# Two-layer graph network: the attention loops written out, gathers that read their row numbers in place, and a small POOL clear after every eight gathers of the second layer

## The chip, the cores and the metric

The kernel runs on one core of one Trainium2 chip. The metric is the device time of one execution in microseconds (us); the number for the kernel before is the median of three runs.

## The reference, cut to what matters

6250 nodes with 64 values each, 200,000 edges (`src`, `dst`, sorted by `dst`), and 64 values per edge. Two layers, each behind a layer norm and a ReLU.

```python
# layer 0: attention over each edge in both directions (400,000 directed edges, 4 heads of 16)
gl, gr = (h @ Wl.T)[src2].reshape(-1, 4, 16), (h @ Wr.T)[dst2].reshape(-1, 4, 16)
score = (att * leaky_relu(gl + gr, 0.2)).sum(-1)
alpha = softmax of score over the edges of one src2 node
out   = segment_sum(gr * alpha[:, :, None], src2)
x = x + gelu(concat(out, h) @ W1.T + b1) @ W2.T + b2
# layer 1: messages
msg = h[src] + edge_attr_64
agg = segment_sum(msg, dst)
x = x + batch_norm(relu(agg @ W1 + b1) @ W2 + b2)
```

Each layer needs one row of 64 values (256 bytes) per edge, picked by a row number that is known only at run time: `gr[dst2]` in layer 0, `h[src]` in layer 1.

## The kernel before, in words

The program is a row of blocks (`prepare`, `sort`, `decode`, `attention`, `attention_nodes`, `messages`, `message_nodes`), written engine by engine with semaphores set by hand. The first three sort the directed edges by node and write the row numbers of all edges into the tile `m.row_of` (128 partitions, one column for each tile of 128 edges), and tables of rows (`gr_table`, `gl_table`) into DRAM. The change touches `attention`, `messages`, and two helpers.

**attention.** 3328 tiles of 128 edges stand in 416 steps of 8 tiles, and the steps in 13 chunks of 32. Step q goes through these hands:

- POOL (line 827) issues 8 indirect DMAs (gathers). Each fetches 128 rows of `gr_table` into `rows[k]`, k = q mod 8 (`U = GATHER_SLOTS = 8` buffers). The row numbers come from `stage[k]`, a small tile of 8 columns.
- SP (lines 837, 842, 843, 851, 858) loads the places of the edges (`place_b`) and the two blocks of left rows (`gl_step`), whose number it reads into a register (L842), reads back the gathered rows of the step 32 earlier (`rows_again`), and, when the 8 gathers of step q have landed, stores them to DRAM (`gr_rows`, L858).
- PE (L882) builds the left rows of each edge with a one-hot matmul, 8 f32 matmuls per step, and for the step 32 earlier sums weighted rows into 8 bf16 matmuls of 204 columns (L889). Its last matmul of step q counts up `s_step`.
- DVE waits for `s_step` and for the gathers, adds left and right rows (L1030, `fore`, counts up `s_z`), weighs the rows of the chunk before (L1035), adds PE's sums into `acc` (L1017), builds one-hots (L1005, L1053), and reduces to scores (L136). Between L1056 and L1062 stands L1009: it copies the 8 row numbers of step q + 7 from `m.row_of` to `stage[(k - 1) % U]` and counts up `s_staged`.
- ACT casts (L967, L969).

Between two chunks DVE, PE and ACT run a scan over the chunk's scores (softmax maxima), lines 1072 to 1135. A step with a score part and a sum part (chunks 1 to 12) is the full one.

POOL may start the gathers of step q when three things have come: the store of step q - 8 has landed (`s_store[k]`), DVE has added the rows of step q - 8 (`s_z` at least q - 7), and DVE has staged the row numbers of step q (`s_staged` at least q + 1):

```python
at_least(pool, s_store[k], j * 16)
at_least(pool, s_z, q - U + 1)
pool.wait_ge(s_staged, q + 1)
```

The steps stand in loops of the hardware: `walk` writes chunks 0 and 1 out and puts chunks 2 to 12 in one loop; `loop` writes the first 8 steps of a chunk out and puts the other 24 in an inner loop of 3 turns. Semaphore values and slices depend on loop registers. POOL has one loop of 51 turns of 8 steps.

**messages.** 1568 tiles of 128 edges stand in 98 groups of 16 tiles, each in two halves of 8 (196 halves). Python loops write all of it out already; only the few groups whose edges reach past one block of nodes run a small loop of the hardware (L1369, L1433). For half h, POOL issues 8 gathers (L1337) from `h2_table` into `rows[h mod 6]` (`U = 6`), with the row numbers in `stage[k]`. It waits for DVE's message of half h - 6 (`s_message` at least h - 5) and for `s_staged` at least h + 1. DVE stages the numbers of half h + 5 (L1386) just ahead of the message of half h (L1421, gathered rows + edge rows), and adds PE's sums into `agg` (L1399, and L1443 in the small loop). PE's matmuls are at L1358, ACT's casts at L1379 and L1381.

## Time and profile before

| | us |
|---|---|
| median of three runs | 9004.02 |
| the three runs | 8930.97, 9004.02, 9032.82 |
| the profiled execution | 9012.64 |
| its span, first to last instruction | 9010.8 |
| first to last gather of attention (L827) | 1127.5 to 6308.1 |
| first to last gather of messages (L1337) | 6676.0 to 8907.0 |
| POOL busy / DVE busy / PE busy | 5385.2 / 5072.6 / 2933.2 |

A time stands for one engine's instruction from start to end. "Idle before" is the time that the engine stood still ahead of it, and what follows `<-` is who ended that. "issue" means that the engine waited for nothing the profile shows, "remote" that the semaphore's sender could not be matched. SPq rows are DMAs issued by SP. The span and the profiled execution differ by 1.84 us, which lie outside the program's own instructions.

### The profile page before, as it was taken

Reading aid. Unit: us, or ns where it says so; the run is one execution under the profiler, and the core shown is the slowest. Engines: PE = TensorE matmul, PEld = TensorE weight load, DVE = VectorE, ACT = ScalarE, POOL = GpSimd, SP = SyncE. Lnnn points to the kernel's source line nnn. Section 1 sums busy time; section 2 is a strip of 40 time slices with the busy share of each in tenths; the row PEclk is TensorE's granted clock in tenths of the full one; section 3 lists DMA queues with packets and bytes.
Section 4 is the critical chain, followed back from the end, with each engine's and each line's share of the span. In section 5 each row is a group of like instructions: output and inputs, shape, how many; then the busy total and the mean of one; then the engine's idle time right before and its main releaser. Section 6 shows DMA issues by size and latency. Waiting matters only on the chain. (4 is left out here: it accounts for less than half of the span.)

```text
span 9010.8 us, 65938 instructions
## 1 busy us (share of the span) xinstructions
PE 2933.2 (33%) x13731; PEld 2480.9 (28%) x13731; DVE 5072.6 (56%) x7913; ACT 1027.4 (11%) x1576; POOL 5385.2 (60%) x4913
## 2 busy tenths in 40 slices
PE   1011122533544333354444334343341112121223
PEld 1011122423434333353333334343220111111112
DVE  9999922745756565575656556564832323333334
ACT  3001100101111111011111101010210101001101
POOL 0000066767777776777777776777036666667774
PEclk9975555555555555555555555555555555555555
DMA  1000022323433333343333333337311111111211
GB/s 30 0 0 0 9 73 65 104 74 85 107 92 93 90 87 85 83 109 91 86 90 88 87 87 91 87 95 71 69 38 44 47 45 48 44 46 46 48 44 31
DMA packets 530967, 588.05 MB, mean 65 GB/s; under 512 B 274126, under 2 KB 277326, under 8 KB 530466
## 3 DMA queue, kind: packets, MB, share of 16 engines
q1 hardware_dynamic: 370066, 421.03, 15.4%
q0 software_dynamic: 156672, 160.75, 11.6%
q10 hardware_dynamic: 3984, 3.89, 0.2%
q14 instruction: 199, 1.63, 0.1%
q8 instruction: 46, 0.75, 0.0%
HBM read 467.65 MB, written 117.55 MB: 65 GB/s over the span
## 5 line engine op out<-in xcount | busy, mean ns | idle before, releaser
L827 POOL DMA_INDIRECT rows<-gr_table,stage x3328 | 3799.1, 1142 | 2345.4 <-DVE stage L1009 1319.7
L882 PE MATMUL bank<-gl_step,hot_t 128*128 128x64 f32 x6720 | 1562.6, 412 | 2205.7 <-issue 1395.0
L882 PEld LDWEIGHTS bank<-gl_step,hot_t 128*128 128x128 f32 x6720 | 1503.1, 327 | 2335.4 <-issue 1660.5
L1337 POOL DMA_INDIRECT message<-h_table,edge_stage x1568 | 1565.3, 998 | 781.8 <-issue 663.3
L1030 DVE TENSOR_TENSOR fore<-bank,rows 128x512 f32<-128x512 f32 x416 | 283.7, 682 | 1472.0 <-remote 803.5
L1358 PE MATMUL bank<-edge_parts,edge_hot 128*128 128x192 bf16 x1568 | 286.4, 363 | 1789.1 <-DVE edge_parts L1428 1201.5
L889 PE MATMUL bank<-parts,hot_sum 128*128 128x204 bf16 x3328 | 681.5, 374 | 484.0 <-issue 403.1
L1358 PEld LDWEIGHTS bank<-edge_parts,edge_hot 128*128 128x128 bf16 x1568 | 202.7, 140 | 1872.7 <-DVE edge_parts L1428 1259.7
L889 PEld LDWEIGHTS bank<-parts,hot_sum 128*128 128x128 bf16 x3328 | 508.3, 159 | 587.1 <-issue 451.0
L967 ACT CAST parts<-terms 128x544 bf16<-128x544 f32 x416 | 268.5, 645 | 2978.7 <-DVE terms L1038 1804.0
L1053 DVE TENSOR_TENSOR hot_sum<-iota_row,place 128x1024 bf16<-128x1024 f32 x416 | 504.5, 1213 | 6.8 <-issue 6.7
L1035 DVE TENSOR_TENSOR terms<-rows_again,weights 128x512 f32<-128x512 f32 x416 | 282.6, 679 | 314.2 <-DMA rows_again<-gr_rows 297.2
L1399 DVE TENSOR_TENSOR agg<-agg,bank 128x192 f32 x98 | 33.8, 345 | 685.0 <-remote 565.9
L1017 DVE TENSOR_TENSOR acc<-acc,bank 128x204 f32 x832 | 297.2, 357 | 175.9 <-issue 93.4
L1443 DVE TENSOR_TENSOR agg<-agg,bank 128x192 f32 x48 | 17.0, 354 | 612.7 <-remote 547.4
L969 ACT CAST parts<-wide 128x544 bf16<-128x544 f32 x416 | 268.4, 645 | 749.0 <-issue 538.6
L607 PE MATMUL bank<-ident,keys 128*128 128x128 f32 x448 | 96.0, 404 | 785.1 <-DVEq L593 697.9
L1379 ACT CAST edge_parts<-bank 128x512 bf16<-128x512 f32 x196 | 114.9, 586 | 1818.9 <-DVE bank L1421 1056.3
L1005 DVE TENSOR_SCALAR hot_t<-place_b,iota_node 128x1024 f32<-128x1024 bf16 x420 | 314.5, 749 | 0.8 <-issue 0.8
L607 PEld LDWEIGHTS bank<-ident,keys 128*128 128x128 f32 x448 | 86.5, 216 | 795.6 <-DVEq L593 703.7
L1050 DVE TENSOR_TENSOR wide<-terms,parts 128x544 f32<-128x544 f32 x416 | 296.9, 714 | 15.2 <-issue 12.2
L1062 DVE TENSOR_TENSOR parts<-wide,parts 128x544 bf16<-128x544 f32 x416 | 296.1, 712 | 0.0
(267 smaller groups left out, 4355.4 us busy)
## 6 DMA issues: line engine op xcount, KB each, us to landing
place_b<-place_rows SPq DMA_DIRECT2D x422, 256.0 KB
gr_rows<-rows SPq DMA_DIRECT2D x416, 256.0 KB
rows_again<-gr_rows SPq DMA_DIRECT2D x416, 256.0 KB
rows<-gr_table,stage POOLq DMA_INDIRECT x3328
edge<-in_edge_attr SPq DMA_DIRECT2D x97, 512.0 KB
gl_step<-gl_table SPq DMA_DIRECT2D x844, 32.0 KB
message<-h_table,edge_stage POOLq DMA_INDIRECT x1568
pen_s<-pen_rows ACTq DMA_DIRECT2D x56, 64.0 KB
```

What stands on the lines that cost most here:

```text
L827: pool.indirect_dma_start(rows[k][:, g, :], None, m.gr_table[:, :], bass.IndirectOffsetOnAxis(stage[k][:, g:g + 1], 0)).then_inc(s_gath[k] ...
L882: last = pe.matmul(bank[slot % LAG][:, g * D:(g + 1) * D], hot_t[slot % LAG][:, g * P:(g + 1) * P], gl_s[slot][:, g // GROUP_TILES, :], st ...
L889: last = pe.matmul(sums_of(slot, g // GROUP_TILES), hot2[slot][:, g, :], parts[slot][:, g, :, :].rearrange("p w f -> p (w f)"), start=g % ...
L1005: dve.tensor_scalar(hot_t[slot][:, :], place_b[place_slot][:, :], m.iota_node[:, 0:1], None, ALU.is_equal).then_inc(s_hot, 1)
L1017: dve.tensor_tensor(sums, sums, sums_of(slot, i), ALU.add).then_inc(s_acc, 1)
L1030: dve.tensor_tensor(z[:, :, :], bank[k % LAG][:, 0:SW].rearrange("p (g f) -> p g f", f=D), rows[k][:, :, :], ALU.add).then_inc(s_z, 1)
L1035: dve.tensor_tensor(terms[:, :, 0:DH], rows2[k % V][:, :, :].rearrange("p g (h f) -> p (g h) f", f=DH), weight.unsqueeze(2).to_broadcast([ ...
L1050: dve.tensor_tensor(rest[:, :, :], terms_by_tile, parts[k % LAG][:, :, 0, :], ALU.subtract).then_inc(s_rest, 1)
L1053: dve.tensor_tensor(hot2[k % LAG][:, :, :], places, at, ALU.is_equal)
L1062: dve.tensor_tensor(parts[k % LAG][:, :, 2, :], rest[:, :, :], parts[k % LAG][:, :, 1, :], ALU.subtract).then_inc(s_parts, 1)
L1337: pool.indirect_dma_start(rows[k][:, e, :], None, m.h2_table[:, :], bass.IndirectOffsetOnAxis(stage[k][:, e:e + 1], 0)).then_inc(s_gath[k] ...
L1358: done = pe.matmul(out[:, 0:3 * D], one_hot[:, e, :], parts[h % 4][:, e, :, :].rearrange("p w f -> p (w f)"), start=first and e == 0, stop ...
```

## The change

1. In `attention` the loops of the hardware are gone: Python loops write out all 416 steps (and the 13 scans) on every engine. Waits compare with constants, slices are fixed. One load of penalties past the last chunk goes too (4 small DMAs of ACT).
2. In both layers the gathers read their row numbers where they lie, one column of `m.row_of` or `m.src`. The `stage` tiles, DVE's copies (L1009, L1386, 423 and 196 of them) and the waits for `s_staged` are gone. The waits for `s_z`, `s_store` and `s_message` stay.
3. In `messages` POOL, after the 8 gathers of each half, clears 256 columns of a spare tile `idle_tile` (128 partitions, f32) that nobody reads: 196 clears. Ahead of each stands a wait on `s_pool`, which POOL itself counts up.

```diff
@@ class Chain
-        self.eng.wait_ge(self.sem, self.turns + self.n)
+        self.eng.wait_ge(self.sem, self.n)
@@ build
+        m.idle = sb("idle_tile", [P, 256], F32)
@@ attention
-    stage = [sb(f"stage{k}", [P, STEP_TILES], I32, ctx) for k in range(U)]
...
-    def loop(eng, part, body):
-
-        body(part, part.c * outer, True)
-        with eng.Fori(part.c * outer + 1, part.c * outer + outer) as j:
-            body(part, j, False)
+    def loop(part, body):
+
+        for i in range(outer):
+            body(part, part.c * outer + i, i == 0)
...
-        for c in range(2):
-            turn(Part(c))
-        with eng.Fori(2, CHUNKS) as c:
-            turn(Part(c))
-        turn(Part(CHUNKS))
+        for c in range(CHUNKS + 1):
+            turn(Part(c))
@@ attention, POOL
-                    pool.wait_ge(s_staged, q + 1)
                     pool.sem_inc(s_pool, 1)
                     for g in range(STEP_TILES):
+                        tile = q * STEP_TILES + g
                         pool.indirect_dma_start(rows[k][:, g, :], None, m.gr_table[:, :],
-                                                bass.IndirectOffsetOnAxis(stage[k][:, g:g + 1], 0)).then_inc(s_gath[k], 16)
-            body(0)
-            with pool.Fori(1, CHUNKS * outer) as j:
+                                                bass.IndirectOffsetOnAxis(m.row_of[:, tile:tile + 1], 0)
+                                                ).then_inc(s_gath[k], 16)
+            for j in range(CHUNKS * outer):
                 body(j)
@@ attention, DVE
-                        at_least(dve, s_gath[(k - 1) % U], (j + (k > 0)) * 16 * STEP_TILES)
-                        stage_of((k - 1) % U, q + U - 1).then_inc(s_staged, 1)
@@ messages, POOL
                 at_least(pool, s_message, h - U + 1)
-                pool.wait_ge(s_staged, h + 1)
                 pool.sem_inc(s_pool, 1)
                 for e in range(HALF):
+                    tile = h * HALF + e
                     pool.indirect_dma_start(rows[k][:, e, :], None, m.h2_table[:, :],
-                                            bass.IndirectOffsetOnAxis(stage[k][:, e:e + 1], 0)).then_inc(s_gath[k], 16)
+                                            bass.IndirectOffsetOnAxis(m.src[:, tile:tile + 1], 0)).then_inc(s_gath[k], 16)
+                pool.wait_ge(s_pool, STEPS + 2 * h + 1)
+                pool.memset(idle[:, 0:256], 0.0).then_inc(s_pool, 1)
@@ messages, DVE
-                    if h + U - 1 < HALVES:
-                        at_least(dve, s_gath[(h - 1) % U], ((h - 1) // U + 1) * 16 * HALF)
-                        stage_of((h - 1) % U, h + U - 1).then_inc(s_staged, 1)
```

DVE, one full step in attention's loop, before:

```order
L1030 TENSOR_TENSOR fore<-bank,rows 128x512
L1035 TENSOR_TENSOR terms<-rows_again,weights 128x32x16
L1038 COPY terms<-weights 128x32
L1005 TENSOR_SCALAR hot_t<-place_b,iota_node 128x1024
L1044 SCALAR_TENSOR_TENSOR fore<-fore 128x512
L1050 TENSOR_TENSOR wide<-terms,parts 128x544
L1053 TENSOR_TENSOR hot_sum<-iota_row,place 128x1024
L1056 TENSOR_TENSOR wide<-fore,att_sb 128x512
L1009 TENSOR_SCALAR stage<-row_of 128x8
L1062 TENSOR_TENSOR parts<-wide,parts 128x8x68
L136 TENSOR_REDUCE scores<-wide 128x32
```

DVE, the same step in the changed kernel (line numbers are its own):

```order
L1016 TENSOR_TENSOR fore<-bank,rows 128x512
L1021 TENSOR_TENSOR terms<-rows_again,weights 128x32x16
L1024 COPY terms<-weights 128x32
L998 TENSOR_SCALAR hot_t<-place_b,iota_node 128x1024
L1030 SCALAR_TENSOR_TENSOR fore<-fore 128x512
L1036 TENSOR_TENSOR wide<-terms,parts 128x544
L1039 TENSOR_TENSOR hot_sum<-iota_row,place 128x1024
L1042 TENSOR_TENSOR wide<-fore,att_sb 128x512
L1045 TENSOR_TENSOR parts<-wide,parts 128x8x68
L136 TENSOR_REDUCE scores<-wide 128x32
```

The staging copy is gone, ninth of the eleven; all else keeps its place.

SP, the first two thirds of one full step in attention's loop, before (ISA rows set registers):

```order
L851 ISA
L851 DMA rows_again<-gr_rows 128x512
L837 ISA
L837 DMA place_b<-place_rows 128x1024
L842 ISA
L842 TENSOR_LOAD blk_i
L842 ISA x2
L843 ISA
L843 DMA gl_step<-gl_table 128x64
L842 ISA
L842 TENSOR_LOAD blk_i
L842 ISA x2
```

SP, the whole of the same step in the changed kernel:

```order
L844 DMA rows_again<-gr_rows 128x512
L830 DMA place_b<-place_rows 128x1024
L835 TENSOR_LOAD blk_i
L835 ISA x2
L836 ISA
L836 DMA gl_step<-gl_table 128x64
L835 TENSOR_LOAD blk_i
L835 ISA x2
L836 ISA
L836 DMA gl_step<-gl_table 128x64
L851 DMA gr_rows<-rows 128x512
```

SP's DMAs keep their order; 18 of its instructions in such a step become 13, since registers no longer count the loop.

POOL, the end of the second layer, before, with what each row waits for:

```order
L1337 DMA message<-h_table,edge_stage 128x64 x7
L1337 DMA message<-h_table,edge_stage 128x64 [waits s_message,s_edge_staged]
L1337 DMA message<-h_table,edge_stage 128x64 x7
L1337 DMA message<-h_table,edge_stage 128x64 [waits s_message,s_edge_staged]
L1337 DMA message<-h_table,edge_stage 128x64 x7
```

POOL, the same place in the changed kernel:

```order
L1313 DMA message<-h_table,src_sb 128x64 x7
L1316 MEMSET idle_tile 128x256 [waits s_pool]
L1313 DMA message<-h_table,src_sb 128x64 [waits s_message]
L1313 DMA message<-h_table,src_sb 128x64 x7
L1316 MEMSET idle_tile 128x256 [waits s_pool]
```

A clear stands between each 8 gathers and the next; the wait for DVE's message of six halves earlier stays at the first gather of each eight.

## Rows read from the trace of the kernel before

**Rows 1.** The page: span, and busy time of each engine.
```profile
span 9010.8 us, 65938 instructions
PE 2933.2 (33%) x13731; PEld 2480.9 (28%) x13731; DVE 5072.6 (56%) x7913; ACT 1027.4 (11%) x1576; POOL 5385.2 (60%) x4913
```

**Rows 2.** Groups of instructions: count | busy us, mean ns | idle before, releasers.
```profile
L827 POOL DMA_INDIRECT rows<-gr_table,stage x3328 | 3799.1, 1142 | 2345.4 <-DVE stage L1009 1319.7 <-issue 1025.1 <-DVE fore L1030 0.3
L1337 POOL DMA_INDIRECT message<-h_table,edge_stage x1568 | 1565.3, 998 | 781.8 <-issue 663.3 <-DVE edge_stage L1386 118.5
...
L1009 DVE TENSOR_SCALAR stage<-row_of 128x8 int32 (+1 forms) x423 | 77.6, 185 | 4.1 <-issue 3.5 <-PEq L646 0.5
```

**Rows 3.** Stretches: length, then each engine's busy time (instructions), clock, DMA share, GB/s.
```profile
1602.00:6308.00 4706.00, 2005.78 (x9312) 1775.86 (x9312) 2817.61 (x5257) 539.54 (x809) 3492.86 (x3016) 0.50 0.37 90
...
6676.00:8907.00 2231.00, 409.36 (x2288) 303.32 (x2288) 761.33 (x1148) 225.08 (x384) 1565.30 (x1568) 0.51 0.19 46
```

**Rows 4.** Waits of POOL: waited for, us in total, times, longest.
```profile
POOL rows L827 <- DVE stage L1009: 1319.7, 25, 963.9
POOL rows L827 <- issue: 1025.1, 3301, 9.5
POOL message L1337 <- issue: 663.3, 1559, 14.9
...
POOL message L1337 <- DVE edge_stage L1386: 118.5, 9, 116.1
```

**Rows 5.** Waits of DVE.
```profile
DVE fore L1030 <- remote: 803.5, 33, 58.2
DVE agg L1399 <- remote: 565.9, 24, 33.8
DVE agg L1443 <- remote: 547.4, 32, 38.0
```

**Rows 6.** Timeline of attention around one stop of POOL: start, length, engine.
```profile
3016.16 0.27 PE L882 MATMUL bank<-gl_step,hot_t 128*128 128x64 f32 x1 [2.53 <-issue]
3016.27 0.95 POOL L827 DMA_INDIRECT rows<-gr_table,stage  x1 [0.31 <-issue]
...
3020.37 0.69 DVE L1030 TENSOR_TENSOR fore<-bank,rows 128x512 f32<-128x512 f32 x1 [42.01 <-remote]
...
3025.86 0.16 DVE L1009 TENSOR_SCALAR stage<-row_of 128x8 int32 x1
...
3026.20 0.35 SPq L858 DMA_DIRECT2D gr_rows<-rows  x1
...
3026.80 0.95 POOL L827 DMA_INDIRECT rows<-gr_table,stage  x1 [9.58 <-DVE stage L1009]
```

**Rows 7.** Timeline of attention where DVE is busy, gathers of POOL.
```profile
3040.13 2.35 POOL L827 DMA_INDIRECT rows<-gr_table,stage  x1 [0.30 <-issue]
3042.79 0.95 POOL L827 DMA_INDIRECT rows<-gr_table,stage  x1 [0.30 <-issue]
```

**Rows 8.** Timeline of messages around one stop of POOL.
```profile
7486.88 2.74 PE L1358 MATMUL bank<-edge_parts,edge_hot_more 128*128 128x192 bf16 x16 [1.70 <-issue]
...
7517.96 0.95 POOL L1337 DMA_INDIRECT message<-h_table,edge_stage  x1 [0.30 <-issue]
7524.54 0.35 DVE L1443 TENSOR_TENSOR agg<-agg,bank 128x192 f32 x1 [37.71 <-remote]
...
7524.89 0.69 DVE L1421 TENSOR_TENSOR bank<-message,edge 128x512 f32<-128x512 f32 x1
...
7525.75 0.95 POOL L1337 DMA_INDIRECT message<-h_table,edge_stage  x1 [6.84 <-issue]
```

**Rows 9.** POOL's clears and the row behind, start to end of the program.
```profile
0.72 0.20 POOL L334 MEMSET ident<- 128x128 f32 x1 [0.29 <-POOLq L1594]
...
6547.80 7.93 POOL L1192 MEMSET agg<- 128x9408 f32 x1
6555.69 4.21 POOL L1193 CAST dst_f<-dst_sb 128x1568 f32<-128x1568 int32 x1
```

**Rows 10.** DVE at the turn of a chunk loop.
```profile
3171.36 1.01 DVE L1133 COPY weights<-bank 128x512 f32<-128x512 f32 x1 [1.89 <-issue]
3175.47 0.69 DVE L1030 TENSOR_TENSOR fore<-bank,rows 128x512 f32<-128x512 f32 x1 [3.11 <-issue]
```

More of the change, by code:

```diff
@@ L102, in __init__ @@
     def __init__(self, eng, sem):
-        self.eng, self.sem, self.n, self.turns = eng, sem, 0, 0
+        self.eng, self.sem, self.n = eng, sem, 0
     def link(self, ins):
@@ L865, in turn @@
             def turn(part):
-                loop(sp, part, body)
+                loop(part, body)
                 if part.score:
@@ L870, in turn @@
                     sp.sem_inc(s_sp, 1)
-            walk(sp, turn)
+            walk(turn)
             for q in range(STEPS + LAG + 2 - V, STEPS + LAG + 2):
@@ L940, in turn @@
             def turn(part):
-                loop(pe, part, body)
+                loop(part, body)
                 if part.score:
                     scan(part)
-            walk(pe, turn)
+            walk(turn)
         def half_of_weights(i):
@@ L973, in turn @@
                 if part.sum:
-                    loop(act, part, body)
+                    loop(part, body)
                 if not part.score:
@@ L1006, in hot_of @@
                                   ).then_inc(s_hot, 1)
-            def stage_of(k, q):
-                return dve.tensor_scalar(stage[k][:, :], m.row_of[:, bass.ds(q * STEP_TILES, STEP_TILES)], 0.0, None,
-                                         ALU.add)
             def accumulate(r, slot, i):
@@ L1023, in body @@
                     tile = q * STEP_TILES - part.c * CHUNK_TILES
-                    if not isinstance(tile, int):
-                        tile = nc.s_assert_within(tile, 0, CHUNK_TILES - STEP_TILES, skip_runtime_bounds_check_because=
-                                                  "a chunk's steps are its tiles")
                     dve.wait_ge(s_step, q + 1)
@@ L1135, in scan @@
                 dve.wait_ge(s_weights_act, c + 1)
-            for k in range(U - 1):
-                stage_of(k, k).then_inc(s_staged, 1)
             chain.link(dve.memset(m.acc[:, :, :, :], 0.0))
@@ L1149, in turn @@
                 c = part.c
-                loop(dve, part, body)
+                loop(part, body)
                 if part.sum:
@@ L1157, in turn @@
                 if part.score:
-                    before = chain.n
-                    if not isinstance(c, int):
-                        chain.turns = (c - 2) * SCAN_LINKS
                     scan(part)
-                    if part.sum:
-                        assert chain.n - before == SCAN_LINKS, chain.n - before
-            walk(dve, turn)
+            walk(turn)
 def attention_nodes(m, ctx):
@@ L1305, in messages @@
     edge = [sb(f"edge{k}", [P, 2, HALF, D], F32, ctx) for k in range(V)]
-    stage = [sb(f"edge_stage{k}", [P, HALF], I32, ctx) for k in range(U)]
     hot = [sb(f"edge_hot{k}", [P, HALF, P], BF16, ctx) for k in range(4)]
@@ L1319, in messages @@
     s_rel = sem("s_dst_rel")
+    idle = m.idle[:, :]
     def steps_before(eng, g):
@@ L1384, in _ @@
         def _(dve):
-            def stage_of(k, h):
-                return dve.tensor_scalar(stage[k][:, :], m.src[:, h * HALF:(h + 1) * HALF], 0.0, None, ALU.add)
             def hot_of(out, numbers, to, n):
@@ L1399, in add_first @@
                 dve.tensor_tensor(sums, sums, bank[g % 2][:, 0:3 * D], ALU.add).then_inc(s_agg, 1)
-            for k in range(U - 1):
-                stage_of(k, k).then_inc(s_staged, 1)
             dve.tensor_copy(bank[3][:, 0:P], m.iota_row[:, :]).then_inc(s_rel, 1)
```

17 lines of the change are left out of this document (7 added, 10 removed).

## Prediction

> **What bounds the kernel now.** I read the page first [rows 1]: POOL and DVE are busy for 5385 and 5073 of 9011 us, neither all through. The stretches [rows 3] say where: from 1602 to 6308 POOL is busy for 3493 of 4706 us and DVE for 2818, in messages POOL for 1565 of 2231 and DVE for 761. So POOL's 4896 gathers lead both layers, and the groups [rows 2] give their price: 1142 ns each in attention, 998 in messages, with 0.30 us ahead of nearly each. Undisturbed, a gather takes 0.95 us and the next starts 0.30 later, 1.25 in all [rows 6]. Beside a busy DVE some take up to 2.35 [rows 7], which is where the 1142 comes from.
>
> The waits of POOL [rows 4] split its idle time. Attention: 1319.7 us on DVE's staging, of which 963.9 is the wait for the first row of all; that leaves 355.8 us in 24 stops, mean 14.8. The 3301 short ones are the 0.30 of issue, 1025 us. Messages: 663.3 us in 1559 waits; 1559 x 0.302 = 471 is issue, so about 192 us are stops, plus 2.4 on L1386. Together 550 us of stops, 6% of the run, are what parts 1 and 2 of the change can touch.
>
> What makes a stop shows in the timelines. In attention [rows 6] DVE stood still for 42 us ahead of L1030, PE meanwhile crawled (one f32 matmul, then 2.53 us of "issue"), and POOL ran on through the steps that it had leave for, until 3017.2. DVE woke at 3020.4, but POOL only at 3026.8, because the staging copy is the ninth of DVE's eleven operations of the step and came at 3025.9. In messages [rows 8] PE's last matmul ended at 7489.6 and DVE, which needs only that sum, went on at 7524.5, 35 us later and 5.6 us after POOL had stopped. So while POOL issues gathers back to back, PE's work and its signals reach others late, DVE waits (803.5, 565.9 and 547.4 us in 89 waits, [rows 5]), and POOL runs out of free buffers. Two readings fit: the delay ends by itself after 20 to 40 us, or POOL's stop is what ends it. 56 of the waits are in messages, 1113 us of them against 194 us of stops: many delays pass while POOL runs on. That speaks for the first. DVE woke 3.2 us and 5.6 us after a stop in the two pieces shown; that speaks for the second.
>
> **The change, part by part.**
>
> *Staging gone from DVE.* 423 + 196 copies of some 0.18 us [rows 2]. DVE is not the bound, and the copy overlaps its neighbours: 0 us on the path.
>
> *Direct indices.* The same 128 numbers of one column are read from another tile: 0 us; bounds -0.02 to +0.02 us a gather from the spread of 0.94 to 0.95 in undisturbed ones, so -98 to +98 us at the very ends; the pattern of the read is alike, so I take 0.
>
> *The staged wait gone, attention.* It does two things. POOL restarts with DVE's L1030 and not with the copy: 3025.86 less 3020.37 is 5.5 us a stop [rows 6], 24 x 5.5 = 132 us. And its leave reaches further: standing at the rows of step q', DVE has staged up to q' + 6, but `s_z` allows q' + 7. That is one step more, 8 x 1.25 = 10 us. What is late next is SP's store, issued at 3026.2, 9 us after the stop, and needed for the step after. Of the 356 - 132 = 224 us that remain, I let a third go (75), between none (second reading) and nearly all (first). Left: about 149. Gain 207; bounds 90 (the store takes over: 3.8 x 24) and 311 (45 left).
>
> *The staged wait gone, messages.* L1421 comes right behind the copy, so the restart gains nothing; the leave grows by one half, 10 us, against stops of 6.84 and the like [rows 8]. I let half of 194 go: 97; bounds 20 and 184.
>
> *The loops written out.* The registers go from the waits: SP issues 13 instructions a step in place of 18. SP crawls with PE, so this can only help its store; counted as nothing. At the turn of a chunk DVE loses 3.11 us to "issue" [rows 10], 11 turns, 34 us, beside POOL's gathers: 0 on the path. The scans and their chains are the same.
> The Trainium skill (Runtime: NRT & Kernel Launch, Instruction fetch mechanics) says that the sequencer fetches straight code ahead, mostly hidden, and that a taken branch out of the window stalls. By it written-out code costs nothing, and the 34 us on DVE go. The row agrees with its stall; that straight code is free POOL's own stream shows, 0.30 us between gathers in messages, which was written out already.
>
> *The clears.* The trace has two POOL clears [rows 9]: 128 columns 0.20 us, 9408 columns 7.93, so 0.84 ns a column, and 256 columns about 0.31 us. Ahead of a gather stands 0.30 us of issue; behind a clear a plain row starts without a gap. If the gather's issue runs under the clear, a clear costs next to nothing; if it is added on both sides, 0.31 + 0.30 + 0.1 for the wait = 0.7. I take 0.45, nearer the clear's own length: 196 x 0.45 = 88 us. Bounds 0 and 137. The wait on `s_pool` is for POOL's own counts, given ten us earlier, and is met.
> The Trainium skill (GPSIMD Engine Reference, Instruction dispatch) says that each of POOL's cores starts its share of the next instruction when its own share of this one is done, and (the same page, When to use GPSIMD) that a pair of cores makes the descriptors. By that most of a clear would run beside the gather, and the 88 would fall toward 0. No row here has a clear between gathers.
>
> *The sum.* 9012.6 - 207 - 97 + 88 = 8797. The median of the runs shown is 8.6 below the profiled one, so 8788; I say 8790. Tail, nodes and sort are untouched.
>
> **The rivals.**
>
> *The delays end by themselves.* Then 10 us more of leave and 5.5 of restart cover a stop of 14.8 nearly whole; 45 us stay for those at the scans. Messages lose 174, pay 88. 9012.6 - 311 - 174 + 88 = 8616, less 9: about 8610. For it: the 56 waits against 194 us. Against: how soon DVE wakes after a stop.
>
> *POOL's stop is what ends them.* POOL then only stops 10 us later, for as long; attention gains the 90 us (store), messages 20, and pay 88: 8991, by the runs about 8980. For it: PE crawls evenly until POOL stops [rows 6]. By the same mechanism the clear is time in which PE may catch up, which would take something off the 88.
>
> *Slower: the clears are paid in full and buy nothing.* Place: POOL in messages. Price 0.7 us each, 137 us, on an engine that is already the bound there, and stops as long as before, since a half now takes longer too. Attention gives nothing, as SP's store and PE's crawl replace the staged wait one for one. 9012.6 + 137 = 9150, by the runs 9140. It decides from where attention gains under 50 us. Against: the 5.5 us of restart are sure in each stop where the store is not late.
>
> *The change does what it says:* the order of POOL and DVE shows no stage and 196 clears, so I give no chance to the contrary.
>
> **How the numbers follow.** The forecast 0.42, ending by themselves 0.22, ending by the stop 0.20, slower 0.16. A measurement of this kernel tells about 1% from no change: the runs before lie 1.1% apart. 1% of 9004 is 90 us, so faster means under 8914. The forecast and the first rival are there nearly whole, little of the second: 0.62. Within 1%: the second rival and the near part of the last, 0.23. Slower 0.15. The forecast's own range is 8690 to 8900. For 8 in 10 it runs from just below the first rival, 8570, past the second, to 9060.
>
> **What would show it.** POOL's gathers in attention span 5181 us now; right would be about 4970, with waits of POOL on SP's store or L1016 adding to some 150 us in place of 356, and each restart within a microsecond of DVE's add. Messages should span about 2222 us, each clear 0.3 us, with no more than half the stops. Stops as many and as long as before would show the second rival; a gap of 1 us or more around each clear, the third; attention gathers with gaps beyond 0.30 every 100 or so would show that straight code isn't free. If DVE's waits ahead of L1016 go away altogether, the delay was tied to the loops, which I don't expect.

## The result, and the profile after

The changed kernel took 8909.05 us (median of 20 runs, 8840.98 to 8993.17) against 8971.78 for the kernel before, 20 runs beside it. The ratio is 0.9916, 95% interval 0.9893 to 0.9940, taken over the runs within 1.5% of the fastest of the same kernel (15 and 19 of the 20). That is 0.8% faster where 2.4% was forecast, and 8909 lies above the forecast's range of 8690 to 8900. Two later series gave 0.9942 (0.9914 to 0.9970) and 0.9971 (0.9940 to 1.0001), so the gain is under 1%, and in the last of them it can't be told from none.

The page of the changed kernel, against [rows 1]:

```profile
span 8908.4 us, 55865 instructions
...
PE 2851.5 (32%) x13731; PEld 2444.8 (27%) x13731; DVE 5009.7 (56%) x7293; ACT 1027.4 (12%) x1576; POOL 5581.5 (63%) x5109
```

Its groups on POOL, against [rows 2] (count | busy us, mean ns | idle before, releasers):

```profile
L820 POOL DMA_INDIRECT rows<-gr_table,row_of x3328 | 3939.9, 1184 | 2111.5 <-issue 2110.9 <-DVE fore L1016 0.6
L1313 POOL DMA_INDIRECT message<-h_table,src_sb x1568 | 1556.8, 993 | 703.6 <-issue 452.7 <-DVE bank L1391 175.7 <-POOLq L1163 75.3
...
L1316 POOL MEMSET idle_tile<- 128x256 f32 x196 | 64.9, 331 | 0.3 <-issue 0.2
```

A stage's length is busy plus idle, less the one long wait for its first row. Attention: 3939.9 + 2111.5 - 963.6 = 5088 us, where [rows 2, 4] give 5181. The idle time fell by 234 us, and 141 came back as longer gathers: the mean went from 1142 to 1184 ns. Messages: 1556.8 + 703.6 - 75.3 + 64.9 = 2250 us, where it was 2231. So the gain is 93 us in attention, less 19 in messages; the rest lies between the layers, where the stretch from the last gather of one to the first of the other went from 368 to 327 us, and behind the last gather, 104 to 116.

The waits of DVE that the prediction rested on, against [rows 5]:

```profile
DVE fore L1016 <- DMA rows<-gr_table,row_of: 1467.5, 290, 8.9
DVE agg L1413 <- remote: 767.9, 33, 53.1
DVE agg L1374 <- remote: 375.3, 15, 37.5
DVE fore L1016 <- remote: 238.3, 10, 40.6
```

A wait on "remote" is called a late signal below: DVE waits for a semaphore whose sender the profile could not match, and by the program that sender is PE. In attention 33 late signals of 803 us became 10 of 238, and DVE now mostly waits for the gathered rows, as it should where POOL leads. All 238 lie before 1650 us, while DVE is in chunk 0 and its scan; the same stretch had 281 before, and what followed it, 523, is gone. In messages nothing changed: 1113 us then, 1143 now.

What the longer gathers are shows in a timeline of POOL and DVE. First the kernel before, around the long gather of [rows 7]:

```profile
3039.84 1.21 DVE L1053 TENSOR_TENSOR hot_sum<-iota_row,place 128x1024 bf16<-128x1024 f32 x1
3040.98 0.68 DVE L1056 TENSOR_TENSOR wide<-fore,att_sb 128x512 f32<-128x512 f32 x1
3041.58 0.16 DVE L1009 TENSOR_SCALAR stage<-row_of 128x8 int32 x1
3041.65 0.71 DVE L1062 TENSOR_TENSOR parts<-wide,parts 128x544 bf16<-128x544 f32 x1
3042.29 0.67 DVE L136 TENSOR_REDUCE scores<-wide 128x512 f32 x1
```

Then the changed kernel at the same point of a step:

```profile
3506.80 1.22 DVE L1039 TENSOR_TENSOR hot_sum<-iota_row,place 128x1024 bf16<-128x1024 f32 x1
...
3507.09 2.98 POOL L820 DMA_INDIRECT rows<-gr_table,row_of  x1 [0.30 <-issue]
3507.93 0.68 DVE L1042 TENSOR_TENSOR wide<-fore,att_sb 128x512 f32<-128x512 f32 x1
3508.54 0.71 DVE L1045 TENSOR_TENSOR parts<-wide,parts 128x544 bf16<-128x544 f32 x1
3509.17 0.68 DVE L136 TENSOR_REDUCE scores<-wide 128x32 f32<-128x512 f32 x1
```

Before, the gather ran from 3040.13 to 3042.48 and ended 0.8 us after L1056, the second of the two-input operations that it ran beside, where the small copy stands. After, it ends at 3510.07, again 0.8 us after the last two-input operation, but that is now the third: nothing stands between L1042 and L1045. The trace before has 43 gathers above 2.5 us in attention, the one after 235. (The Trainium skill, SBUF — State Buffer, Who interferes with whom, says that a DVE instruction with two inputs in SBUF contends with a GpSimd instruction that reads SBUF. The rows agree, and the next section tests it.)

### The profile page after: what moved, and what is told of

The parts are those of the page before. It is cut to its first block and busy times, and to the rows that moved or that the text cites. A ratio compares the mean times of both kernels' runs of the same rounds, so it can differ in the third digit from the quotient of the medians.

```text
span 8908.4 us, 55865 instructions
## 1 busy us (share of the span) xinstructions
PE 2851.5 (32%) x13731; PEld 2444.8 (27%) x13731; DVE 5009.7 (56%) x7293; ACT 1027.4 (12%) x1576; POOL 5581.5 (63%) x5109
## 5 line engine op out<-in xcount | busy, mean ns | idle before, releaser
L820 POOL DMA_INDIRECT rows<-gr_table,row_of x3328 | 3939.9, 1184 | 2111.5 <-issue 2110.9
L875 PEld LDWEIGHTS bank<-gl_step,hot_t 128*128 128x128 f32 x6720 | 1477.1, 329 | 2725.8 <-DVE parts L1045 2155.1
L1313 POOL DMA_INDIRECT message<-h_table,src_sb x1568 | 1556.8, 993 | 703.6 <-issue 452.7
L1016 DVE TENSOR_TENSOR fore<-bank,rows 128x512 f32<-128x512 f32 x416 | 286.1, 688 | 1785.9 <-DMA rows<-gr_table,row_of 1467.5
L882 PE MATMUL bank<-parts,hot_sum 128*128 128x204 bf16 x3328 | 653.2, 377 | 92.9 <-DVE parts L1045 79.7
L1045 DVE TENSOR_TENSOR parts<-wide,parts 128x544 bf16<-128x544 f32 x416 | 296.6, 713 | 0.0
```

What stands on the lines that cost most here:

```text
L820: pool.indirect_dma_start(rows[k][:, g, :], None, m.gr_table[:, :], bass.IndirectOffsetOnAxis(m.row_of[:, tile:tile + 1], 0)).then_inc(s_g ...
L875: last = pe.matmul(bank[slot % LAG][:, g * D:(g + 1) * D], hot_t[slot % LAG][:, g * P:(g + 1) * P], gl_s[slot][:, g // GROUP_TILES, :], st ...
L882: last = pe.matmul(sums_of(slot, g // GROUP_TILES), hot2[slot][:, g, :], parts[slot][:, g, :, :].rearrange("p w f -> p (w f)"), start=g % ...
L1016: dve.tensor_tensor(z[:, :, :], bank[k % LAG][:, 0:SW].rearrange("p (g f) -> p g f", f=D), rows[k][:, :, :], ALU.add).then_inc(s_z, 1)
L1045: dve.tensor_tensor(parts[k % LAG][:, :, 2, :], rest[:, :, :], parts[k % LAG][:, :, 1, :], ALU.subtract).then_inc(s_parts, 1)
L1313: pool.indirect_dma_start(rows[k][:, e, :], None, m.h2_table[:, :], bass.IndirectOffsetOnAxis(m.src[:, tile:tile + 1], 0)).then_inc(s_gath ...
```

## The experiments

Eighteen experiments in six series. The kernels of a series ran one after another on one chip, the kernel before beside them (the expectations say "call" for it). The ratio is always to the kernel before in the same series, since series differ, more than I had thought possible. For the stops of POOL in attention I take the idle time of the row, less the 1978.4 us of a trace in which no stop stands (below): the kernel before had 367 us, the changed one 133. Each trace is of one execution of a kernel, and executions of one kernel lie up to 2% apart.

**First series: pieces of the change.** Without the clears; all loops written out but staging kept; POOL's loop alone written out, with direct indices, staging kept in messages; and the changed kernel with this edit:

```diff
-                        at = m.place[:, ...].unsqueeze(2).to_broadcast([P, STEP_TILES, P])
-                        dve.tensor_tensor(hot2[k % LAG][:, :, :], places, at, ALU.is_equal)
+                        for t in range(STEP_TILES):
+                            col = r * STEP_TILES + t
+                            dve.tensor_scalar(hot2[k % LAG][:, t, :], m.iota_row[:, :], m.place[:, col:col + 1], None, ALU.is_equal)
```

> The changed kernel without the 196 clears of messages; all else is as changed. In the changed kernel's trace a clear lasts 0.33 us and the gap from gather to gather across it is 0.49 us where 0.30 stood before, so theory A (the clears cost 0.19 us each and buy nothing) expects messages shorter by 196 x 0.19 = 37 us, from 2249 to about 2212, and the whole at about 0.4% below the changed kernel (ratio to the kernel before 0.987). Theory B (the clears are a pause in which PE catches up, so they pay for themselves) expects messages as long as or longer than 2249 us, with more or longer stops of POOL than the 24 of 185 us, and the ratio to before at 0.992 or above.

> The kernel before with attention's loops written out on every engine, but with the staging copies and their waits kept in both layers, and no clears. Theory A (writing the loops out is what freed PE and SP: their register work is what crawled while POOL gathered) expects DVE's waits ahead of its first add of a step (803 us on remote senders before) down near the 238 of the changed kernel, attention at 5088 to 5130 us, and a ratio to before of about 0.990. Theory B (the staged wait was what made the stops, as the prediction had it) expects attention at 5130 to 5180 us with some 350 us of stops as before, and a ratio of 0.998 or above.

> The kernel before with POOL's loop alone written out and attention's gathers reading their row numbers in place, no staging in attention; the loops of SP, PE, ACT and DVE stay, messages stay as before. Theory A (the loops of the other engines make the delays) expects DVE's remote waits of some 800 us unchanged, POOL's stops moved from the copy to DVE's add, and attention within 60 us of 5181, ratio 0.994 or above. Theory B (the staged wait) expects attention near 4970 to 5088 us and the ratio near 0.985 to 0.990.

> The changed kernel with DVE's one-hot of the sums (L1039, 128x1024, two inputs in SBUF, 1213 ns) written as 8 operations of 128x128 that each compare one tile with a scalar of each partition; the result is the same. In the changed kernel a gather takes 1184 ns on the mean against 946 beside an idle DVE, 790 us in all. Theory A (the two-input operations hold POOL up, this one for about a third of it) expects the mean at 1100 to 1130 ns and attention shorter by 180 to 280 us, near 4850, if DVE is no slower. Theory B (any busy DVE lengthens a gather, or DVE loses more by eight starts than POOL gains) expects the mean within 20 ns of 1184 and attention within 50 us of 5088 or longer.

The kernel before took 8395 us in this series (13 runs, 8386 to 8440), where it had taken 8972. The four: 8525 (ratio 1.0151, 1.0119 to 1.0184), 8468 (1.0074, 1.0050 to 1.0098), 8466 (1.0084, 1.0053 to 1.0115), 8493 (1.0117, 1.0087 to 1.0146). POOL's groups in the order of the runs, one fence each:

```profile
L820 POOL DMA_INDIRECT rows<-gr_table,row_of x3328 | 3887.8, 1168 | 1978.4 <-issue 1977.8 <-DVE fore L1016 0.6
L1313 POOL DMA_INDIRECT message<-h_table,src_sb x1568 | 1573.8, 1004 | 554.0 <-issue 477.8 <-POOLq L1163 76.2
```

```profile
L837 POOL DMA_INDIRECT rows<-gr_table,stage x3328 | 3809.6, 1145 | 1978.3 <-issue 1013.3 <-DVE stage L1018 964.4 <-DVE fore L1039 0.6
```

```profile
L835 POOL DMA_INDIRECT rows<-gr_table,row_of x3328 | 3852.4, 1158 | 1978.1 <-issue 1978.1
```

```profile
L820 POOL DMA_INDIRECT rows<-gr_table,row_of x3328 | 3780.8, 1136 | 1978.7 <-issue 1975.3 <-DVE fore L1016 3.4
L1315 POOL DMA_INDIRECT message<-h_table,src_sb x1568 | 1622.8, 1035 | 566.2 <-issue 450.4 <-POOLq L1165 115.7
...
L1318 POOL MEMSET idle_tile<- 128x256 f32 x196 | 65.0, 332 | 0.1
```

Idle is 1978 us in all four: 964 for the first row and 0.305 for each other gather. There isn't one stop, nor a late signal on DVE. So the delays don't belong to the kernel alone, and in a series without them the pieces show bare. Dropping the staging copy and its wait made the gathers longer by 3887.8 - 3809.6 = 78 us (39 above 2.5 us became 205), and 8525 - 8468 = 57 us came out. The one-input one-hot took 107 us off against the run without clears, 1136 ns a gather for 1168. That is the direction of its theory A at a smaller size: A had expected 1100 to 1130 ns and at least 180 us. The clears, which of the four only the last has, cost 1622.8 + 566.2 - 115.7 + 65.0 = 2138 less 2052, 86 us: 37 in gaps and 49 in longer gathers (1035 ns for 1004; why they are longer no run shows). None of the expectations foresaw a series without stops; what they say of stops stayed untested here.

**Second series: both kernels again.**

> The kernel before, unedited. In the four runs so far it took 8395 us where it had taken 8972 on the chip of the profile shown, and none of the four kernels had a stop of POOL. Theory A (the stops and the crawl of PE and SP belong to the chip, not to the kernel) expects that on a chip where it takes about 8395 us its trace has no stop of POOL over 0.5 us, gathers of 1130 to 1145 ns in attention, attention at about 4810 us and messages at about 2050; and on a chip where it takes about 8970, some 50 stops of 550 us. Theory B (the delays come with the kernel's own loops) expects stops here, and longer gathers nowhere.

> The changed kernel, unedited. Theory A (what the change gains is only stops; where there are none it only costs) expects on a chip without stops: attention 4902 us, as in the run without clears, messages 2051 + 85 = 2137 as in the run with the one-input one-hot, so some 8580 us, 2.2% above the kernel before. On a chip with stops: a ratio of 0.992 as before. Theory B (the clears pay for themselves) expects messages near 2051.

Delays were back (before 8958 us, 17 runs): 8948 for the profiled run of the kernel before, with 62 stops of 533 us in both layers, 8909 for the changed one, ratio 0.9942. The gathers were as in the first pair, 1143 and 1194 ns. But the stretch between the layers came out the other way round, 322 us before and 375 after. It follows TensorE's granted clock in the nodes' part: first the profiled pair, before and after (columns as in [rows 3]), then the second pair:

```profile
6525.00:6676.00 151.00, 95.84 (x279) 50.44 (x277) 54.69 (x68) 28.37 (x48) 17.44 (x4) 0.50 0.10 22
```

```profile
6470.00:6542.00 72.00, 42.72 (x220) 24.32 (x218) 23.98 (x25) 20.33 (x36) 0.00 (x0) 0.81 0.10 23
```

```profile
6450.00:6606.00 156.00, 73.71 (x368) 44.75 (x368) 97.11 (x143) 42.76 (x71) 17.42 (x3) 0.64 0.16 38
```

```profile
6400.00:6592.00 192.00, 111.62 (x360) 61.12 (x360) 93.39 (x134) 41.76 (x69) 17.42 (x3) 0.50 0.12 30
```

0.50 is the 1.2 GHz level, and 0.81 and 0.64 are stretches partly at 2.4 GHz. The stretches shown are not of equal length or work, but the whole way between the layers tells the same in all twenty traces: at a granted clock of 0.50 it took 361 to 389 us, at 0.57 or 0.58 it took 307 to 335. Either kernel can meet either, so the 41 us there are no part of the change.

**Third series: the gap on DVE.** The changed kernel without clears; the same with one copy put back at the old place, which nobody waits for; with three; and again the written-out, staged one:

```diff
+                        dve.tensor_scalar(m.idle[:, 0:STEP_TILES].bitcast(I32), m.row_of[:, 0:STEP_TILES], 0.0, None, ALU.add)
                         dve.tensor_tensor(parts[k % LAG][:, :, 2, :], rest[:, :, :], parts[k % LAG][:, :, 1, :], ALU.subtract
```

> The changed kernel without the 196 clears, again, as the base of the two spacer runs on the same chip. On a chip where the kernel before takes about 8960 us (chip with delays): theory A (clears cost 0.19 us each beside the stops) expects messages about 37 us shorter than the 2254 us of the changed kernel and a ratio to before of 0.990; theory B (clears pay for themselves) 0.994 or above. On a chip where before takes about 8395: 1.015 again.

> The run without clears plus one DVE operation in each full step of attention: a copy of 128x8 row numbers into a spare tile that nobody reads, at the very place where the staging copy stood (between the weighing of the scores and the parts). Theory C (the staging copy, a one-input operation between two-input ones, was the gap in which a blocked gather got through; without it three two-input operations stand in a row) expects gathers over 2.5 us to fall from some 200 to some 45, the mean gather in attention from about 1170 to 1190 down to 1145, and attention shorter by 75 us where there are no stops and up to 150 where there are. Theory D (the longer gathers come from POOL running without stops, or from the other tile being read) expects no fewer than 180 gathers over 2.5 us and attention within 20 us of the run without the spacer, or longer by the 415 x 0.18 us that DVE works more.

> As the run with one spacer, with two more: one between L1036 and the one-hot of the sums, one behind that one-hot. Theory C expects still fewer long gathers: none over 2.5 us but for the scans, the mean below 1140, attention another 20 to 60 us shorter. Theory D expects it no shorter than without spacers, and DVE's step longer by 3 x 0.18 us, which nobody waits for.

> The kernel before with attention's loops written out on every engine, staging kept, no clears, on the same chip as the spacer runs. Theory C expects gathers of about 1143 ns here, as in the kernel before. On a chip with delays: if writing out freed PE and SP, stops of POOL in attention well under the 345 to 376 us of the kernel before and attention near 5000 us, under both kernels; if it was the staged wait, stops of 345 us again and attention near 5170. On a chip without delays: 4823 us as before.

The chip was the same as in the first series, but the kernel before now took 9107 us (20 runs): the delays don't belong to the chip either. Without clears 8951 us (0.9851, 0.9821 to 0.9882), one spacer 9005 (0.9913, 0.9879 to 0.9947), three 8959 (0.9864, 0.9823 to 0.9905), staged 9041 (0.9911, 0.9878 to 0.9945). Without the spacer, then with one:

```profile
L820 POOL DMA_INDIRECT rows<-gr_table,row_of x3328 | 4003.2, 1203 | 2063.7 <-issue 2063.4 <-DVE fore L1016 0.3
```

```profile
L820 POOL DMA_INDIRECT rows<-gr_table,row_of x3328 | 3806.0, 1144 | 2351.8 <-issue 2351.8
...
DVE fore L1016 <- remote: 921.1, 39, 59.1
```

Theory C's gathers came to the digit: 1144 ns against 1203, 197 us less, 27 above 2.5 us against 285. Yet attention got longer by 91 us (5194 for 5103), since the stops rose from 85 to 373 and DVE's late signals from 258 to 921 us. Theory C had expected it shorter. (The spacer's trace is of the longest of its eight runs, 9080 us; by the medians it is 54 us slower.) This run has no staged wait and no staging, and its stops are those of the kernel before (367). So the stops don't need the staged wait, and they are fewer where the copy is missing and the gathers are longer: every trace with delays, without a copy on DVE and without clears in attention has 56 to 133 us of them (six traces), every one with a copy 270 to 434 (five). Two more spacers made gathers no shorter (1148 ns; the expected fall below 1140 didn't come), with 270 us of stops and attention at 5104 us. The staged one had gathers of 1143 ns as expected, but 434 us of stops and attention at 5253 us, neither the 5000 that freed engines would have given nor the 5170 of the staged wait; its trace is of a run of 9102 us, where the median is 9041.

**Fourth series: what ends a delay.** Changed kernel; without clears; without clears but with 7 message buffers (`U, V = 7, 3`); and this, in both layers, with the spacer:

```diff
+                    for i in range(3):
+                        pool.wait_ge(m.s_pause, ...)
+                        pool.memset(m.rest_tile[:, :], 0.0).then_inc(m.s_pause, 1)
```

> The changed kernel, beside the same without clears, for the price of the 196 clears alone. In a call with delays (the kernel before at 8950 us or more): theory A (a clear costs its gap, 0.19 us) expects it 37 us slower than without clears, 0.4%; theory B (a clear lets PE catch up) expects stops of messages some 40 us less than without (230 us in 30 stops there, 190 in 28 with) and the two kernels within 0.2% of each other. In a call without delays (8395): 85 us slower, messages 2137 against 2051.

> The changed kernel without clears, as the base of the other three. With delays: ratio to before 0.985 to 0.990, attention 5100, messages 2262. Without: ratio 1.015, attention 4902, messages 2051.

> The run without clears with the spacer copy on DVE (short gathers, 1144 ns) and with a pause of POOL of its own: three clears of 248 columns behind each 8 gathers, in attention and in messages, some 1.0 to 1.2 us each time. With delays, theory E (a pause of POOL in each step, of whatever kind, lets PE and SP catch up, so the long gathers did the work that the stops had done) expects POOL's stops in attention to fall from the 382 us of the spacer run to 100 to 150 and in messages from 230 to under 120, DVE's waits with them, while the pauses themselves cost 416 and 196 times 1 us: gaps and stops together about as before, the whole within 2% of the spacer run. Theory F (the missing copy itself, on DVE, is what made the stops fewer) expects the stops unchanged at about 380 and 230 us and the pauses added in full: attention near 5600, messages near 2460. Without delays: attention 4823 + 420, messages 2051 + 200.

> The run without clears with 7 buffers for gathered rows in messages in place of 6, so POOL's leave reaches one half (10 us) further. With delays, theory G (a delay ends by itself, the first rival of the prediction) expects that stops of a mean of 7.7 us go almost wholly: messages 2262 - 180 = about 2080. Theory H (POOL's stop is what ends the delay, the second rival) expects the stops as long as before, only each 10 us later: messages within 30 us of 2262. Without delays there are no stops and nothing changes: 2051.

Before 8943 us (29 runs); 8910 (0.9971), 8914 (0.9959, 0.9932 to 0.9986), pauses 9129 (1.0221, 1.0175 to 1.0268), seven buffers 8904 (0.9957, 0.9928 to 0.9985). The clears neither cost nor bought anything that a measurement tells, and messages lasted 2250 us with them and 2253 without. In their order, POOL's message groups with clears, without, and with seven buffers:

```profile
L1313 POOL DMA_INDIRECT message<-h_table,src_sb x1568 | 1557.4, 993 | 743.3 <-issue 451.2 <-DVE bank L1391 176.4 <-POOLq L1163 115.8
```

```profile
L1313 POOL DMA_INDIRECT message<-h_table,src_sb x1568 | 1564.7, 998 | 804.2 <-issue 474.0 <-DVE bank L1389 214.4 <-POOLq L1163 115.8
```

```profile
L1313 POOL DMA_INDIRECT message<-h_table,src_sb x1568 | 1559.7, 995 | 766.1 <-issue 472.6 <-DVE bank L1389 218.5 <-POOLq L1163 75.0
```

The waits on DVE's message are 176, 214 and 218 us: a clear takes from the stops about what it adds, and a seventh buffer, 10 us more of leave, takes nothing. A delay does not end by itself here; theory G falls. The pauses agree. POOL's groups, then all that is left of DVE's late signals:

```profile
L822 POOL DMA_INDIRECT rows<-gr_table,row_of x3328 | 3757.5, 1129 | 2080.7 <-issue 2080.7
L1319 POOL DMA_INDIRECT message<-h_table,src_sb x1568 | 1575.2, 1005 | 600.7 <-issue 524.4 <-POOLq L1169 76.3
L827 POOL MEMSET rest_tile<- 128x248 f32 x1248 | 390.4, 313 | 48.1
...
DVE agg L1420 <- remote: 4.8, 1, 4.8
```

No stop is left in either layer. What remains over the pauses is a gap of 0.8 us more at every 64th gather of attention, 41 us in all, and 1.2 us more at 19 gathers of messages. Theory E's expectation of 100 to 150 us of stops was too cautious, and theory F is out. A pause makes the gap of 0.305 us one of 1.50 in attention and 1.47 in messages, 416 x 1.20 + 196 x 1.17 = 728 us in all, which is why the kernel is slower all the same.

**Fifth and sixth series: how much of a pause.** With the spacer, one clear behind each 8 gathers of attention and two in messages; without the spacer, one clear in attention and three behind every second half; a third with the spacer; last, the spacer and one clear in attention alone.

> The run with pauses in a smaller dose: the spacer copy on DVE, one clear of 248 columns behind each 8 gathers of attention (gap 0.49 in place of 0.30 us), two in messages (gap about 1.0). Theory E (any pause of POOL lets PE and SP catch up, and less than the 1.5 us of the three clears will do) expects no remote waits of DVE in attention and in messages, attention at 4823 + 79 = 4902 to 4950, messages at 2051 + 133 = 2184 to 2200, and the whole at about 8700, below both kernels by over 2%. Theory F2 (a pause must be long, and one clear buys little, as the changed kernel's messages show) expects stops of attention at 250 us or more, attention at 5150 or more, and messages still short of stops or not according to the length: with two clears, stops of 60 to 150 us and messages at 2250 to 2330.

> No spacer copy, so gathers of some 1200 ns, one clear behind each 8 gathers of attention; in messages three clears behind every second half, so the same pauses as in the run with pauses, half as often. Theory E expects DVE's remote waits ahead of L1016 (250 us) gone, attention at 4902 + 79 + the longer gathers, 5050 to 5100, no better than without clears; in messages no stops and 2051 + 98 x 1.17 = 2166 us if one pause in 20 us is enough, or half the stops, some 110 us, and 2270 if it isn't.

> The spacer copy on DVE, three clears behind every second step of attention, two behind each half of messages. Theory E expects attention without remote waits at 4823 + 208 x 1.17 = 5066 us if one pause in 20 us is enough, and stops of some 190 us and 5250 if it isn't; messages as in the run with one and two clears, 2184 to 2200.

> The run with one spacer copy on DVE plus one clear of 248 columns behind each 8 gathers of attention, and nothing in messages; so it differs from the spacer run (0.991, attention 5194 us with 382 us of stops) by the clear in attention alone, and from the run with one and two clears (0.970, attention 4983, messages 2253) by the messages alone. Theory E (the clear in attention is what took the stops) expects attention at 4960 to 5000 us with under 100 us of stops, messages at 2250 to 2265 with 220 us of stops (clears there trade for stops one for one), and a ratio to before of 0.970 with delays. Theory I (the call was a favourable one, and the clear does little) expects attention at 5100 to 5200 and a ratio of 0.985 or above. Without delays: attention 4823 + 79 = 4902, messages 2051, ratio about 1.005.

The kernel of the third was not the one that its expectation describes: it had two clears behind every step of attention and two behind every second half, and it is read so here. Its expectation stays untested. Against 9064 us (11 runs): 8784 (0.9701, 0.9658 to 0.9744), 8977 (0.9894, 0.9851 to 0.9937), 9193 (1.0141, 1.0096 to 1.0186). The last, against 8942 us (11 runs): 8804 (0.9862, 0.9815 to 0.9908). Attention with the spacer and one clear, from the last run:

```profile
L822 POOL DMA_INDIRECT rows<-gr_table,row_of x3328 | 3819.1, 1148 | 1984.6 <-issue 1984.6
...
L827 POOL MEMSET rest_tile<- 128x248 f32 x416 | 134.9, 324 | 0.2
...
DVE fore L1022 <- remote: 284.0, 15, 40.5
```

3819.1 + 1984.6 + 134.9 - 964.4 = 4974 us, in the range that theory E gave, and 220 less than with the spacer alone (5194). The gap across a clear is 0.485 us in place of 0.305, 75 us for all 416, and some 65 us of stops are left where the spacer alone had 373. The two stand in different series and the spacer's trace is a long one, so the 220 are no more than a size: five traces with a copy and no clear have attention at 5104 to 5253 us, the two with a copy and one clear at 4972 and 4983. The ratio points less clearly: 0.986 is what theory I had expected (0.985 or above), not the 0.970 of theory E. In us the two best runs stand 20 apart, while the kernel before took 9064 us beside the one and 8942 beside the other. The clears of messages had no part in that (2253 and 2244 us).

Where the remaining stops lie says more. POOL's first 40 steps fall while DVE is in chunk 0, whose steps have no sum part, and in the scan behind it; the other 376 steps feed the full ones. Stops of POOL in attention, in us, traces with delays:

| kernels (traces) | first 40 steps | the other 376 |
|---|---|---|
| copy on DVE, no clear in attention (5) | 74 to 87 | 192 to 347 |
| no copy, no clear in attention (6) | 51 to 78 | 6 to 63 |
| copy, one clear (2) | 64, 66 | 0 |
| no copy, one clear (1) | 70 | 0 |
| copy, two clears (1) | 6 | 0 |
| copy, three clears (1) | 0 | 0 |

So one clear of 0.32 us behind each 8 gathers ended every stop of the full steps, and nearly every late signal of L1016 or L1022 there. First the spacer alone, then with one clear, both from 1650 us on:

```profile
DVE fore L1016 <- remote: 679.2, 25, 59.1
```

```profile
DVE fore L1022 <- remote: 9.0, 1, 9.0
```

In attention only the first 40 steps needed more than one clear. The fifth series has the comparison within one series, too: the kernels with and without the copy, each with one clear in attention, have the same stops (66 and 70 us), and the copy still saves 185 us of gathers (1150 ns for 1206), 4983 us for 5172.

By dose, with the spacer: attention's stops are 373, 65, 6 and 0 us for 0, 1, 2 and 3 clears (with two and three another 40 us lie in the short gaps at every 64th gather), and DVE's late signals at L1016 or L1022 921, 284, 130 and 0. In messages the late signals are 1232 us without clears, 1143 with one (the changed kernel), 801 with two and 5 with three; but their length is 2253, 2250, 2253 and 2304 us, so there a pause only took the place of a stop. Theory E was too strong in one thing: it expected no late signals at all with one clear in attention and two in messages. Messages kept 801 us of them, and 978 us with three clears behind every second half (2255 us of messages), so there a rarer or shorter pause is a partial cure. Without the spacer, one clear in attention gave 5172 us with gathers of 1206 ns, where 5074 and 5103 had come without a clear: the long gathers had left only 56 to 85 us of stops, 70 stood there with the clear as well, and so its 75 us of gaps are paid in full. Two clears in attention made the gathers longer, 1191 ns, where one gave 1148 and three 1129, and attention 5372 us. How often a gather meets DVE's two-input operations seems to depend on POOL's pace against DVE's step; no run was made to test that.

The two kernels with the spacer and one clear in attention, at 8804 and 8784 us, took 0.986 (0.982 to 0.991) and 0.970 of the kernel before, where the changed one has 0.992 to 0.997. No series held them beside the changed one, and one and the same kernel, the one without clears, had 0.985 in the third series and 0.996 in the fourth; so that they are faster than the changed kernel is likely, and not shown. Without delays they weren't run: from the staged form there, 8468 us, and 75 us of gaps they would come to some 8540, 1.8% above the kernel before (an estimate).

## Why the forecast missed, and what it had right

The step that failed first is the price of 0 for the copy that goes from DVE: the gathers beside it got longer, +141 us in the profiled pair. The second is the 97 us that messages should have gained, where nothing went.

- *Staging gone from DVE, 0 us.* This step failed. I priced the copy by DVE's time. It was the one-input operation between two-input ones in which a blocked gather got on; without it a gather costs 1184 to 1204 ns in place of 1143, +141 us in the profiled pair, 78 in the series without delays. I had the collision in [rows 7] and both operation lists, and didn't ask what the copy did for POOL.
- *The staged wait, attention, -207.* The idle time fell by 234, so the size was right and the reason wrong. With the wait gone and a copy kept the stops were 373 us; neither the 132 of restarts nor the 10 of further leave is to be seen in them, and the ratio (0.9913) was that of the staged form (0.9911). (The 3.8 us a stop behind the lower bound of 90 stand in no row.) The stops went with the copy. The likely reason is that longer gathers are a pause of POOL in each step, as a clear is: clears ended the stops with the copy in place. That the longer gathers work in that way is argued, not shown.
- *The staged wait, messages, -97.* Wrong. Nothing went: waits of 176 to 229 us on DVE's message in every run with delays and direct gathers but those with longer pauses, and a seventh buffer changed nothing. I had taken a middle between two readings; the second, that POOL's stop ends the delay, is the one that the seventh buffer and the pauses bear out, and it gives 0.
- *The clears, +88.* 86 in the series without delays, which is the price I gave, by luck, since the sum is another (37 of gaps, 49 of gathers). With delays about 0, because they are taken out of the stops. The sentence of the second rival, that a clear is time in which PE catches up, was the half that I didn't count.
- *Direct indices 0:* no run separates it from the rest. With the spacer back, direct gathers took 1144 ns, staged ones 1143, so any difference is of the order of 1 ns a gather.
- *Loops written out, 0.* Open. Staged and written out, the kernel was 0.7% slower than before without delays and 0.9% faster with them; no trace of the kernel before stands in either series. With delays that is more than half of the 1.5% by which the kernel without clears was faster in the same series, so the 0 may be a failed step too; which term it went through no run shows.
- *The sum.* The forecast -207 - 97 + 88 = -216 came as -234 + 141 + 19 = -74; the other 28 us of the 102 by which the span fell are TensorE's clock between the layers (-41) and the tail (+12). The delays behaved as in the second rival, where POOL's stop ends them, and the forecast had taken a middle way. Its 90 us for attention came out (93) by luck, on another way; its messages, +68, came as +19. What I had called a sign against me, DVE's late signals ahead of L1016 going, came for two thirds (all of them outside the first 40 steps), but not by the loops: with the loops written out and the spacer in place all are back (921 us).

## What to carry to other kernels

Before removing a small operation from one engine, look at what stands on both sides of it and which other engine they hold up: its worth can be the gap. While an engine issues gathers back to back, the signals of others can come late. A pause that widened one gap in eight by 0.2 us cost 75 us and ended the 192 to 347 us of stops in the full steps of one layer, and bought nothing in the other; so try the dose and read the waiting engine's late signals. Where a kernel's time differs by 8% between series, compare only within a series, and take the traces of more than one.

## What I had not expected of the hardware

- The same kernel before took 8395 us in one series and 8942 to 9107 in all others, once 8395 and once 9107 on the same chip. For the kernel without clears traces of both kinds exist: attention 4902 and messages 2052 us without a late signal, 5103 and 2263 with them. Of the 201 us in attention 85 are stops and 115 are longer gathers (1168 and 1203 ns); the 211 in messages are stops. What makes the delays stays open, and so does why the gathers lengthen with them.
- PE's signals reach DVE up to 60 us late while POOL issues gathers, and a pause of POOL ends that. Three clears (a gap of 1.5 us) behind each 8 gathers ended all but 5 us of it in both layers; one clear (0.49 us) did so in the full steps of attention, and hardly anything in messages (1143 us for 1232). Which resource PE and POOL share there no run shows.
